# Constant rows of the first stacks by ScalarE and VectorE, those of the second sent later, first x in one transfer

## What is computed

```
x = L0_attn_x                                  # [16, 512, 256] float32
xn = _layernorm(x, axis=-1)
# attention: 16 heads of 16, causal, q/k/v/o weights [256, 256]
q, k, v = (proj(Wq), proj(Wk), proj(Wv))
scores = jnp.einsum('bhsd,bhtd->bhst', q, k)
scores = jnp.where(mask, -jnp.inf, scores)
attn = jax.nn.softmax(scores / sqrt(D), axis=-1)
out = jnp.einsum('bhst,bhtd->bhsd', attn, v)
s = jnp.einsum('bse,fe->bsf', out, Wo)
# ffn: int32 weights times 1/127, hidden 768
h = _silu(jnp.einsum('bsd,hd->bsh', xn, wg)) * jnp.einsum('bsd,hd->bsh', xn, wu)
g = _silu(jnp.einsum('bsh,dh->bsd', h, wd))
x = x + s * g
```

## Time and profile before

| | us |
|---|---|
| median of 3 runs | 975.44 |
| lowest, highest | 973.7, 975.92 |
| the profiled execution, its own time | 980.97 |
| its span in the profile | 979.3 |
| TensorE busy | 935.7 |
| VectorE busy | 705.2 |
| ScalarE busy | 578.9 |
| GpSimd busy | 493.9 |

### The profile page before, as it was taken

One profiled execution on the slowest core, in us unless ns is written; L12 is line 12 of the kernel. 1 busy time (PEld: TensorE's weight loads), 2 busy tenths in 40 slices (PEclk: granted clock), 3 DMA queues, 4 the chain that ended last, 5 costly groups with the idle time before them and its releaser, 6 DMA issues.

```text
span 979.3 us, 22676 instructions
## 1 busy us (share of the span) xinstructions
PE 935.7 (96%) x9034; PEld 691.7 (71%) x9034; DVE 705.2 (72%) x949; ACT 578.9 (59%) x793; POOL 493.9 (50%) x672
## 2 busy tenths in 40 slices
PE   5569999999999999999999999999999999999995
PEld 4457767686776768686776867777686877768655
DVE  6577775968777786868778587777868677786833
ACT  4125566656666575666657566665756666575672
POOL 4015534654646455464645546464554746455453
PEclk9779999999999999999999999999999999999997
DMA  8422315435343443534344353434535343443323
GB/s 246 173 68 100 121 56 180 140 121 171 125 153 113 170 151 121 167 122 159 109 165 152 124 169 123 157 110 169 152 121 167 122 158 110 173 146 123 122 80 104
DMA packets 86123, 135.01 MB, mean 138 GB/s; under 512 B 13568, under 2 KB 36352, under 8 KB 86016
## 3 DMA queue, kind: packets, MB, share of 16 engines
q1 hardware_dynamic: 86016, 133.52, 41.0%
HBM read 53.22 MB, written 25.75 MB: 81 GB/s over the span
## 4 chain that ended last, share of the span: by engine, by line
PE 77%; issue 5%; DMA 5%; POOL 4%; ACT 4%; DVE 4%; SPq 1%; ACTq 0%; POOLq 0%; DVEq 0%
PE bank L192 41%; PE values L525 11%; PE bank L430 11%; PE bank L492 8%; PE bank L443 4%; ACT probs L500 2%; POOL o_compact L566 2%; DMA mean_and_rstd<-scratch_m 1%; DMA o_reciprocals<-scratch_r 1%; DMA scratch_r<-sum_reciprocals 1%; ACT o_hi L573 1%; DVE row_max L455 1%; DVE gated L375 1%; SPq L318 1%; DMA scratch_m<-mv 1%
## 5 line engine op out<-in xcount | busy, mean ns | idle before, releaser
L455 DVE TENSOR_REDUCE row_max<-bank 128x2 f32<-128x768 f32 (+3 forms) x352 | 384.6, 1124 | 70.6 <-PE bank L443 66.4
L500 ACT ACTIVATE probs<-bank 128x1024 f32<-128x1024 f32 x320 | 319.9, 1024 | 125.3 <-PE bank L492 125.1
L507 POOL TENSOR_SCALAR_AFFINE_SELECT probs<-probs 128x256 f32<-128x256 f32 (+1 forms) x448 | 194.9, 452 | 289.7 <-ACT probs L500 287.2
L430 PE MATMUL bank<-k_stack,q_stack 64*128 64x128 f32 (+3 forms) x1024 | 160.9, 373 | 13.8 <-DMA q_stack<-qk_hi 8.4
L525 PE MATMUL values<-probs,v 128*17 128x512 f32 (+3 forms) x2048 | 166.4, 436 | 1.5 <-POOL probs L507 1.2
L389 POOL TENSOR_TENSOR h_lo<-gated,h_hi 128x512 fp32r<-128x512 f32 x96 | 124.3, 1296 | 56.5 <-ACT h_hi L386 54.3
L492 PE MATMUL bank<-q_stack,k_stack 64*128 64x512 f32 (+3 forms) x1024 | 142.8, 352 | 6.3 <-issue 5.3
L430 PEld LDWEIGHTS bank<-k_stack,q_stack 64*128 64x128 f32 x1024 | 86.5, 190 | 82.6 <-issue 40.4
L492 PEld LDWEIGHTS bank<-q_stack,k_stack 64*128 64x128 f32 x1024 | 83.1, 186 | 47.1 <-issue 23.8
L362 DVE SCALAR_TENSOR_TENSOR gated<-gated,bank 128x512 f32<-128x512 f32 x96 | 65.7, 685 | 52.3 <-ACT gated L359 52.3
L443 PE MATMUL bank<-causal_mask,half_identities_bf 64*128 64x128 bf16 (+3 forms) x1408 | 100.8, 228 | 0.0
(11 more groups left out here) (114 smaller groups left out, 1642.0 us busy)
## 6 DMA issues: line engine op xcount, KB each, us to landing
k_stack<-qk_hi SPq DMA_DIRECT2D x64, 256.0 KB, 2.5
q_stack<-qk_hi SPq DMA_DIRECT2D x64, 256.0 KB, 2.6
scratch_o<-o SPq DMA_DIRECT2D x64, 256.0 KB, 2.5
k_stack<-qk_lo SPq DMA_DIRECT2D x32, 256.0 KB, 2.5
q_stack<-qk_lo SPq DMA_DIRECT2D x32, 256.0 KB, 2.8
x_again<-x SPq DMA_DIRECT2D x16, 512.0 KB, 4.6
o_compact<-scratch_o SPq DMA_DIRECT2D x32, 256.0 KB
o_reciprocals<-scratch_r SPq DMA_DIRECT2D x32, 256.0 KB
```

What stands on the lines that cost most here:

```text
L430: nc.tensor.matmul(PS[:, n, j * keys:(j + 1) * keys], r(QS[par][low:low + STACK, pair, i * P:(i + 1) * P]), r(KS[par][low:low + STACK, pai ...
L455: signal(e.tensor_reduce(rows, scores, axis=AX.X, op=ALU.max), "d_sm")
L500: signal(e.activation(PR[:, (SCORES * beta + k) % SLOTS, :, :], both(banks), ACT.Exp, scale=SCALE_S), "d_ex")
L507: last = e.affine_select(out=diag, in_=diag, compare_op=ALU.is_ge, fill=0.0, base=0, pattern=[[0, many], [1, P]], channel_multiplier=-1)
```

## The change

Line 284 in the kernel before is 285 after, 318 is 321, 430 is 433.

- x of the first batch is one DMA of 512 KB with one semaphore, in place of four DMAs of 128 KB.
- The constant rows of `k_stack0` and `q_stack0` no longer come by DMA. VectorE fills the first half of `k_stack0` with ones (whole partitions, 2048 elements each) as its first instruction. ScalarE fills `q_stack0` with zeros in two activations and the second half of `k_stack0` with ones in a third, ahead of its list. The `ls` DMAs into these stacks wait for the fills.
- The constant rows of `k_stack1` and `q_stack1` still come by two DMAs of 512 KB, now in a unit `rw 0 0`, which stands in `HEAD` behind `ls 0 3`. The first `sm` waits for no fill; that of the second batch does.
- GpSimd fills the zeros and the ones first.

```diff
-    sm 0 10 34, mk 0 10 34, sm 0 11 56, fl 0 0, ls 0 3, mt 0 0 2, gu 0 2 3, sm 0 12 01, mk 0 11 56, gg 0 3 4, mk 0 12 01,
+    sm 0 10 34, mk 0 10 34, sm 0 11 56, fl 0 0, ls 0 3, rw 0 0, mt 0 0 2, gu 0 2 3, sm 0 12 01, mk 0 11 56, gg 0 3 4, mk 0 12 01,
...
-        s_first = [sem(f"s_first{t}") for t in range(TT)]
+        s_first = sem("s_first")
...
+        s_zeros, s_ones, s_kfill, s_qfill = sem("s_zeros"), sem("s_ones"), sem("s_kfill"), sem("s_qfill")
...
-                    if beta == 0:
-                        e.wait_ge(s_first[t], 16)
+                    if beta == 0 and t == 0:
+                        e.wait_ge(s_first, 16)
                     last = e.bn_stats(STATS[:, t, :], XIN[:, t, :])
...
+                if beta == 0:
+                    e.wait_ge((s_kfill, s_qfill)[k % 2], m + 1)
                 stack, order = ((KS[par], (0, 0, 1)), (QS[par], (0, 1, 0)))[k % 2]
                 for n, part in enumerate(order):
                     e.dma_start(stack[n:P:4, half, :], QKP[part][:, k % 2, :]).then_inc(s_stack[k], 16)
...
-                    if half == 0 and beta < 2:
-                        e.wait_ge(s_rows, 64)
-                    elif half == 0:
+                    if half == 0 and beta == 1:
+                        e.wait_ge(s_rows, 32)
+                    elif half == 0 and beta > 1:
...
-                    e.wait_ge(s_rows, 64)
+                    e.wait_ge(s_rows, 32)
...
+        def u_rw(en, e, beta, par, k, banks, prev):
+            if en == "sp":
+                e.wait_ge(s_zeros, 1)
+                e.wait_ge(s_ones, 1)
+                e.dma_start(KS[1][MROW:P:4, :, :], RDEN[0:32, :].rearrange("p (o s) -> p o s", o=1).to_broadcast([32, PAIRS, S]))\
+                 .then_inc(s_rows, 16)
+                e.dma_start(QS[1][MROW:P:4, :, :].rearrange("p a (i s) -> p (a i) s", i=2),
+                            ZERO[0:32, :].bitcast(FP32).rearrange("p (o s) -> p o s", o=1).to_broadcast([32, 2 * PAIRS, 256]))\
+                 .then_inc(s_rows, 16)
...
+            e.memset(ZERO[:], 0.0).then_inc(s_zeros, 1)
+            e.memset(RDEN[:], 1.0).then_inc(s_ones, 1)
             e.memset(IDF[:], 0.0).then_inc(s_const, 1)
             e.memset(IDB[:], 0.0).then_inc(s_const, 1)
             e.memset(MASK[:], 0.0).then_inc(s_const, 1)
-            e.memset(ZERO[:], 0.0).then_inc(s_const, 1)
             e.memset(MINUS_HALF[:], -0.5).then_inc(s_const, 1)
-            e.wait_ge(s_const, 5)
+            e.wait_ge(s_const, 4)
...
-            e.memset(RDEN[:], 1.0).then_inc(s_const, 1)
...
-            for t in range(TT):
-                e.dma_start(XIN[:, t, :], x[0, t * P:(t + 1) * P, :]).then_inc(s_first[t], 16)
+            e.dma_start(XIN[:], x[0].rearrange("(t p) e -> p t e", p=P)).then_inc(s_first, 16)
...
-            e.wait_ge(s_const, 9)
-            for i in range(2):
-                e.dma_start(KS[i][MROW:P:4, :, :], RDEN[0:32, :].rearrange("p (o s) -> p o s", o=1).to_broadcast([32, PAIRS, S]))\
-                 .then_inc(s_rows, 16)
-                e.dma_start(QS[i][MROW:P:4, :, :].rearrange("p a (i s) -> p (a i) s", i=2),
-                            ZERO[0:32, :].bitcast(FP32).rearrange("p (o s) -> p o s", o=1).to_broadcast([32, 2 * PAIRS, 256]))\
-                 .then_inc(s_rows, 16)
             run("sp", e)
...
+            half = PAIRS // 2
+            e.wait_ge(s_zeros, 1)
+            zeros = ZERO[:].bitcast(FP32).rearrange("p (o s) -> p o s", o=1).to_broadcast([P, PAIRS, 256])
+            for m in range(2):
+                e.activation(r(QS[0][:, m * half:(m + 1) * half, :].rearrange("p a (i s) -> p (a i) s", i=2)), zeros, ACT.Copy)\
+                 .then_inc(s_qfill, 1)
+            e.wait_ge(s_ones, 1)
+            e.wait_ge(s_kfill, 1)
+            e.activation(r(KS[0][:, half:, :]), RDEN[:].rearrange("p (o s) -> p o s", o=1).to_broadcast([P, half, S]), ACT.Copy)\
+             .then_inc(s_kfill, 1)
             run("act", e)
 
         @block.vector
         def _(e):
+            e.memset(KS[0][:, 0:PAIRS // 2, :], 1.0).then_inc(s_kfill, 1)
             run("dve", e)
...
-            e.wait_ge(s_const, 8)
-
+            e.wait_ge(s_const, 7)
+            e.wait_ge(s_zeros, 1)
```

More of the change, by code:

```diff
@@ L333, in u_v @@
                 if beta < 2:
-                    e.wait_ge(s_const, 11)
+                    e.wait_ge(s_const, 9)
                 signal(e.activation(V[par][:, 2 * k:2 * k + 2, :, 0:D].rearrange("p t h d -> p (t h) d"),
@@ L450, in u_mk @@
                 if beta == 0:
-                    e.wait_ge(s_const, 12)
+                    e.wait_ge(s_const, 10)
                 at = pairs[0] % (PAIRS // 2)
@@ L666, in u_fl @@
                 e.transpose(PVB[0:1, 0:P], LOW[:, 3:4], IDF[:]).then_inc(s_flag, 1)
-        UNIT = dict(wt=u_wt, ld=u_ld, xr=u_xr, la=u_la, lm=u_lm, lc=u_lc, lt=u_lt, lb=u_lb, lx=u_lx, tr=u_tr, qk=u_qk, ls=u_ls, v=u_v, gg=u_gg, gu=u_gu, hs=u_hs,
+        UNIT = dict(rw=u_rw, wt=u_wt, ld=u_ld, xr=u_xr, la=u_la, lm=u_lm, lc=u_lc, lt=u_lt, lb=u_lb, lx=u_lx, tr=u_tr, qk=u_qk, ls=u_ls, v=u_v, gg=u_gg, gu=u_gu, hs=u_hs,
                     fl=u_fl, dn=u_dn, sm=u_sm, mk=u_mk, mt=u_mt, zr=u_zr, st=u_st, pv=u_pv, od=u_od, ob=u_ob, on=u_on, os=u_os, op=u_op)
```

## The result

| | before | after |
|---|---|---|
| median, first comparison (7 runs each) | 973.78 us | 967.70 us |
| ratio, 95% interval | | 0.9929 (0.9912 to 0.9946) |
| median, repeated (11 and 6 runs) | 976.94 us | 968.68 us |
| ratio, 95% interval | | 0.9921 (0.9902 to 0.9941) |
| span of the profiled execution | 979.3 us | 966.1 us |

The change makes the kernel faster by 6 to 8 us, 0.7 to 0.8%. The forecast was 9.6 us less (965.8 us), with a range of 962.5 to 971.0. By its time alone the first comparison (6.1 us less) can't be told from the prediction's rival A (5.4 to 8.5 us less); the profile decides.

What follows compares the result with a forecast made beforehand. TensorE, busy 96% of the span, was taken as the bound, losing 8.36 us in the head waiting for the query stack. Gains of 8.3 + 1.3 = 9.6 us, subtracted from the median, gave 965.8 us, range 962.5 to 971.0.

Steps and rivals of the forecast that it cites:

- rival A: Program start: VectorE's fill and GpSimd's constants hold each other up; gain only 5.4 to 8.5 us; chance 0.13.
- The wait and its cause: Before the first raw scores: fills delay the stack DMAs; with them gone TensorE's 8.36 us wait goes altogether.
- Rival B: Stack DMAs: 178 GB/s belongs to transfers into the stacks, not the fills; gain about 4.5 us, 971.0; chance 0.05.
- VectorE next: Behind the stacks VectorE is late next: first row maximum 8.3 us earlier, `gated` L375 9.6 us earlier.
- the better case: TensorE's clock behind the first scores stays at the upper level; gain 11.1 to 11.3 us in all.
- The fills on the engines: Program start: ScalarE's three fills at most 5.9 us, VectorE's at most 2.3; cost 0, with x at most 0.2 us.
- The later fills: SyncE's queue: two moved fills issued around 33 to 35 us, over by 43, maxima at about 49; cost 0.
- Rival D: SyncE's queue: moved fills delay the maxima, `st 0 0` starts 2.6 us later than before; 978.0 us; chance 0.02.
- I subtract the same 9.6 from the median: Whole kernel: the 9.6 us gain worked out on the profiled execution is taken off the median too, giving 965.8.
- the worse case of the clock: TensorE's clock falls to the lower level after idling some 2 us from about 27.5; gain 9.6 us.

Runs made afterwards that it cites:

- experiment 2: Kernel before with one or two of four DMA fills moved behind the stack DMAs: 972.64, 967.24 us; kernel after with two left ahead: 968.29 us.
- experiment 4: Kernel after with the three reductions of the weights' lo parts moved from VectorE to ScalarE; median 966.63 us, ratio to before 0.9904.
- second profile: Kernel before run and profiled once more, no edit; profiled execution 975.57 us, median 976.16 us, ratio 1.0009.
- later_only: Kernel before with only the second stack's two DMA fills moved behind the fourth group of stack DMAs; median 967.24 us, ratio 0.9918.
- before_busy: Kernel before with 34 useless matmuls of zeros on TensorE in its wait for the stacks; median 974.66 us, ratio 0.9989 (0.9974 to 1.0003).
- three_ahead: Kernel before with one of four DMA fills (zeros of the second query stack) moved behind the fourth group of stack DMAs; median 972.64 us, ratio 0.9973.
- four_x: Kernel after with the first x in four transfers again; 967.86 us, ratio to before 0.9913.
- one_x: Kernel before with the first x in one transfer and nothing else changed; 975.01 us, ratio 0.9997.
- flag_act: The kernel of experiment 4: kernel after with the lo parts' reductions as sums of absolute values on ScalarE; median 966.63 us, ratio to before 0.9904.

## Why the prediction was right, and where not

**The wait and its cause: right.** TensorE's wait went whole (24.39, forecast 24.7 to 25.5), SyncE is not held up, and the dose of experiment 2 shows the fills as the cause; how much of it is their transfer and how much the issues that they block stays open. Rival B (the stack DMAs slow by themselves) is out: they landed in 2.5 us. The fills, with nothing but stack DMAs ahead, still needed 7.2 and 8.4 us: the slowness belongs to the fills.

**VectorE next: right.** The maxima start at 26.06 (forecast 26.6), L378 at 28.32 (28.95), both without idle time; experiment 4 shows TensorE as the next one behind it.

**The clock: the better case came.** The point forecast took the lower level after the 2 us gap at 27 us; the granted clock stayed at 1.00 until 36, and against the first profile the shift grew to 11.5 us (at the first store of `o` 11.1), as worked out for that case (11.1 to 11.3).

**The fills on the engines: right.** ScalarE's three took 5.6 us (bound 5.9), VectorE's is 1.76 us in its row (bound 2.3), and rival A did not occur at the fills: VectorE's fill ran beside GpSimd's constants, and the power came 0.2 us late, the upper bound given. The mechanism of rival A did occur at a place that the prediction doesn't look at: the casts, in two profiles, at 1.1 and 1.2 us. It has no term for the earlier sending of the weights and doesn't ask which engine that would wake.

**The later fills: right.** Issued at 34.4 and 35.2, landed at 43.6, the maxima at 46.1. Rival D is out, though the margin, 2.5 us, was smaller than I had thought (over by 43, maxima at about 49).

**The term that was mis-sized is the last one: "I subtract the same 9.6 from the median".** The medians moved by 6.1 and 8.3 us. The size is that of one execution, and the slowest seen. The second profile, whose time lies at the median, has a wait of 7.3 in place of 8.4 and the lower clock only half as long. Against it the kernel after is ahead by 8.4 us at the first store of `o` (83.17, 74.79), and by 7.7 us in the span (973.8, 966.1). The difference of 0.7 us and the rest down to the 6 to 8 us of the medians are of the size by which executions differ behind the head. From the last store of `o` to the end it takes 22.7 us in the second profile of before and 24.7 in that of after, but 24.0 in the first profile of before and 22.4 in `later_only`: this varies with the execution and not with the kernel. So the 9.6 belongs to the profiled execution (measured there: 11.1 to 11.5 in the head), and a usual one is worth about 8. That the forecast of 965.8 lies within 2 us of 967.70 is in part luck: the point forecast took the worse case of the clock, which made the gain smaller, and a wait longer than usual, which made it larger.

**Open:** how much of the 2 to 4 us of clock behind the wait a usual execution of before really pays, since `before_busy` is faster by only 1.1 us with an interval up to none (`three_ahead` and `later_only` put 1.7 us on it in their profiles); and whether the casts' overlap explains why the kernel after (0.9921 to 0.9929) is not ahead of `later_only` (0.9918) and `four_x` (0.9913). The intervals overlap.

## What to carry to other kernels

Constants that must be in place before the first real work compete with it for the DMA queue even when each is small work. Send first what is read first; what only the second iteration reads can go behind, and that alone brought all of the gain that the times can tell here, before any engine was given fills to do.

When a wait has a length in one profiled execution, look at how that execution's time stands among the others before taking the length as the gain: here the wait for the busy queue was 8.4 us in one profile and 7.3 in the next, and the clock behind it differed too.

When something arrives earlier, ask what it wakes: here an earlier weight let GpSimd's cast fall into VectorE's critical instruction.

## What the runs showed of the hardware that I had not expected

- A DMA fill of 32 partitions in steps of four, 512 KB from a broadcast source, landed in 7.2 and 8.4 us with only stack DMAs and each other in the queue, while a stack DMA of 256 KB into the same kind of rows took 2.5. By the rows the two fills together (1.05 million bytes, 34.43 to 43.6) went at some 115 GB/s, the three stack DMAs of the first queries (0.79 million, 20.31 to 24.0) at some 210.
- The time at which four such fills let the stacks through differed by execution: TensorE's first scores started at 32.25, 33.07, at 30.91 where they were sent 1.8 us sooner (`one_x`), and, with useless work in the wait, at 34.97.
- VectorE's fill of 2048 float32 per partition has a row of 1.76 us, 0.86 ns an element. The Trainium skill ("VectorE: DVE Perf Modes", "Zero memsets can be issued as uint32 (trn2)") has one cycle per element, an estimate of 2.1 us at its 0.96 GHz; the row is shorter. But it starts at 1.30 where the other engines start at 0.80, so it may have begun before its record.
- A sum along the row on ScalarE by its accumulator costs 0.19 us beside the 1.48 us of the activation over 1536 elements (`flag_act`).
